# Scatter of token rows to expert slots held to two transfers under way, and one more shared block placed ahead of the expert loop

## What is computed

```python
logits = x_flat @ gate_w.T
scores = jax.nn.softmax(logits, axis=-1)
_, topk_ids = jax.lax.top_k(scores, 2)
w = scores * jax.nn.one_hot(topk_ids, E).sum(axis=1)
gu = jnp.einsum('nh,eih->nei', x_flat, experts_gate_up)
g, u = (gu[..., :I], gu[..., I:])              # I = 352, E = 8
h = jax.nn.silu(g) * u
expert_out = jnp.einsum('nei,ehi->neh', h, experts_down)
out = jnp.einsum('neh,ne->nh', expert_out, w)
shared = jax.nn.silu(x_flat @ shared_gate_w.T) * (x_flat @ shared_up_w.T) @ shared_down_w.T
shared_weight = jax.nn.sigmoid(x_flat @ shared_expert_gate_w.T)
out = out + shared_weight * shared             # width of shared: 704
# caller: x = x + tanh(g_ffn[1]) * out
```

## Time and profile before

| | us |
|---|---|
| median of three runs | 1020.92 |
| lowest and highest | 1019.35, 1020.96 |
| the profiled execution, whole | 1029.16 |
| its span, first to last instruction | 1027.0 |
| PE busy in it | 950.7 (93%) |
| DVE, ACT, POOL busy | 578.8, 482.1, 582.9 |
| mean granted TensorE clock | 0.966 |

### The profile page before, as it was taken

How to read it: one execution, slowest core, us unless ns; L and a number is a source line. 1 busy time by engine, 2 the same in 40 slices (tenths; PEclk the granted TensorE clock), 3 DMA queues, 4 the chain that set the end, 5 groups by cost and what they waited for, 6 DMA issues and landing times. The chain is left out here.

```text
span 1027.0 us, 21395 instructions
## 1 busy us (share of the span) xinstructions
PE 950.7 (93%) x7715; PEld 539.4 (53%) x7716; DVE 578.8 (56%) x1698; ACT 482.1 (47%) x661; POOL 582.9 (57%) x620
## 2 busy tenths in 40 slices
PE   6989999999996998988999999997994999999997
PEld 2644444444473554644444444464552677777754
DVE  4867888888752115776888888846331222222226
ACT  2437787887833111436877778744010122322210
POOL 3458999999834701378999999941066022222200
PEclk9978999999998998989999999998998999999999
DMA  9572838374002161464343424122722022222152
GB/s 305 183 219 44 227 64 226 65 209 82 2 22 83 43 214 37 123 138 128 64 114 64 109 54 104 27 86 110 228 78 104 17 62 62 67 62 64 44 174 82
DMA packets 87988, 107.56 MB, mean 105 GB/s; under 512 B 10528, under 2 KB 70520, under 8 KB 87896
## 3 DMA queue, kind: packets, MB, share of 16 engines
q1 hardware_dynamic: 77192, 85.08, 30.3%
q0 software_dynamic: 4848, 14.70, 4.3%
q10 hardware_dynamic: 5856, 6.56, 2.1%
HBM read 76.92 MB, written 29.38 MB: 104 GB/s over the span
## 5 line engine op out<-in xcount | busy, mean ns | idle before, releaser
L616 ACT ACTIVATE pT<-ps 128x1024 f32<-128x1024 f32 x256 | 248.4, 1022 | 98.8 <-PE ps L488 98.5
L658 POOL TENSOR_TENSOR xT<-nmax,xT 128x512 f32<-128x512 f32 x192 | 195.5, 1040 | 21.6 <-DVE nmax L556 21.3
L658 POOL TENSOR_TENSOR s<-nmax,s 128x512 f32<-128x512 f32 x192 | 196.5, 1040 | 16.8 <-DVE nmax L556 12.6
L556 DVE CUSTOM_DVE_ANT_0 s<-ps,bias 128x512 f32<-128x512 f32 x256 | 166.1, 689 | 45.2 <-PE ps L475 43.9
L556 DVE CUSTOM_DVE_ANT_0 xT<-ps,bias 128x512 f32<-128x512 f32 x256 | 166.5, 689 | 42.6 <-PE ps L475 32.3
L475 PE MATMUL ps<-ks,qs 97*128 97x512 bf16 (+1 forms) x512 | 162.5, 397 | 12.2 <-DMA ks<-qk_scratch 4.6
L503 PE MATMUL ps<-pT,vq 128*32 128x512 f32 x1024 | 135.5, 605 | 2.4
L1182 POOL DMA_INDIRECT slots_out<-y,id x39 | 38.2, 980 | 138.6 <-DVE y L1509 135.3
L475 PEld LDWEIGHTS ps<-ks,qs 97*128 97x128 bf16 (+1 forms) x512 | 30.6, 98 | 131.4 <-DVE nmax L556 65.1
L1261 PE MATMUL ps<-gu,xgT 128*128 x312 | 98.8, 460 | 0.7 <-ACT xgT L1345 0.7
L1212 PE MATMUL ps<-xT,sgu 128*128 128x512 f32 x176 | 81.2, 617 | 15.0 <-issue 10.1
(11 more groups left out here) (173 smaller groups left out, 1215.4 us busy)
## 6 DMA issues: line engine op xcount, KB each, us to landing
bias<-in_bias SPq DMA_DIRECT2D x16, 1024.0 KB, 5.9
qk_scratch<-parts SPq DMA_DIRECT2D x64, 128.0 KB
qs<-qk_scratch SPq DMA_DIRECT2D x32, 192.0 KB, 3.3
ks<-qk_scratch SPq DMA_DIRECT2D x32, 192.0 KB, 4.0
gu<-in_gate_up SPq DMA_DIRECT2D x8, 704.0 KB, 9.6
slots_in<-zeros POOLq DMA_DIRECT2D x4, 1280.0 KB, 7.1
xg<-slots_in SPq DMA_DIRECT2D x39, 130.0 KB, 2.1
qk_scratch<-parts ACTq DMA_DIRECT2D x32, 128.0 KB
```

What stands on the lines that cost most here:

```text
L556: nc.vector.tensor_tensor_reduce(at.s[m % 4][:, qt, :], sb.ps[:, ring_bank(tile_place[u - 1 + hg * 64]), :], at.bias[:, j if per_head_bias ...
L616: nc.scalar.activation(at.pT[:, slot(m // HG, m % HG), 2 * half:2 * half + 2, :], sb.ps[:, 2 + 2 * half:4 + 2 * half, :], ACT.Exp).then_in ...
L658: nc.gpsimd.tensor_tensor(s, at.nmax[:, m % 4, qt:qt + 1].to_broadcast([P, S]), s, ALU.subtract).then_inc(pool_less_max, 1)
```

## The change

`scattered` becomes two semaphores, used in turn. From the third scatter of each round on, POOL waits until the scatter before the previous one has landed, so that at most two are under way. `EARLY` becomes 2: block (1,1) moves from the late to the early ones.

```diff
-EARLY = 1
+EARLY = 2
...
-    slots_ready, scattered = sem("slots_ready"), sem("scattered")
+    slots_ready, scattered = sem("slots_ready"), [sem(f"scattered{i}") for i in range(2)]
...
-            sp.wait_ge(scattered, 16 * 2 * TT)
+            for i in range(2):
+                sp.wait_ge(scattered[i], 16 * TT)
...
             for c in range(2):
                 if c == 1:
-                    pool.wait_ge(scattered, 16 * TT)
+                    for i in range(2):
+                        pool.wait_ge(scattered[i], 16 * TT // 2)
...
                 for t in range(TT):
+                    if t >= 2:
+                        pool.wait_ge(scattered[t % 2], 16 * (c * TT // 2 + t // 2))
                     pool.indirect_dma_start(
                         out=scr.xs, out_offset=bass.IndirectOffsetOnAxis(ap=m.slot[:, c, t:t + 1], axis=0),
-                        in_=sb.tok[:, t, :], in_offset=None).then_inc(scattered, 16)
+                        in_=sb.tok[:, t, :], in_offset=None).then_inc(scattered[t % 2], 16)
```

## The result

The median of 13 runs of the changed kernel is 1013.84 us (1009.16 to 1017.91), beside 1024.1 us for 13 runs of the kernel before (1019.35 to 1027.51). The ratio is 0.9902, with a 95% interval of 0.9884 to 0.9919: 10 us faster. The forecast was 1013.5 us.

The account below looks back on a forecast made before the run. PE and its late signals during the scatters were taken to bound the stretch before the loop, PE then DVE the end. -3.0 and -8.6 gave -11.6: 1017.6 us, or 1009.4; the middle, 1013.5 us, was forecast, range 1009 to 1027.

Parts of the forecast that it names:

- The sum: Whole kernel: -3.0 us ahead of the expert loop and -8.6 us behind it, -11.6 us together.
- The end: Behind the loop: without block (1,1), DVE's last add moves from 1023.67 to 1015.10, -8.6 us.
- The front: Ahead of the loop: block (1,1) adds 13.8 us, yet without stall the first transpose starts at 807.3, not 810.3: -3.0 us.
- the holes: Idle PE time ahead of the loop that no work fills: 3.22 us at 771.17 and 10.07 us at 784.27.
- the second hole: PE's 10.07 us of idle time at 784.27, after which its granted clock was read as down to 0.50.
- The wait on POOL: Scatter stretch: two scatters take 3.2 us instead of 2.53, `xg` is there at 804.5, PE hides it: cost 0.
- The remark on an estimate of 2.3 us for one transfer: Scatter on POOL: by a fitted formula the wait would be satisfied and `xg` there 1.5 us sooner, hidden by PE.
- From the profiled execution to the median: Whole kernel: 1017.6 us like the profiled execution, or 1009.4 if its excess is spread over all work; middle 1013.5 us.
- the 8.2 us: Whole kernel: how far the earlier kernel's median lay below its profiled execution; either spread over all work or stall.
- The stall is not the scatters' number: Ahead of the loop: something else in that window causes the idle time, which stays; +5.2 us, 1026 us; chance 0.22.
- the likeliest case: Ahead of the loop: limiting scatters under way removes PE's stall; 1013.5 us, own range 1009 to 1018, chance 0.47.
- The stall belongs to the profiled execution: Ahead of the loop: timed runs lack the stall, so the change costs +3.3 us, 1024.2 us; chance 0.15.

Follow-up runs that it names:

- the block alone: Changed kernel without the wait between scatters: block (1,1) early, two semaphores in turn; 1016.03 us (1.0046 to before) on one chip, 1027.69 us (1.0066) on another.

## Why the prediction was right, point by point

**The sum.** -3.0 ahead of the loop and -8.6 behind it were forecast, -11.6; the two traces give -3.0 and -8.5, and the medians -10.3. The first transpose was forecast 57.6 us after the first scatter and came after 57.7.

**The end.** Four `expert_add` at 3.17 us in a row, then 1.7: held to a tenth. DVE now ends last, PE's last down being over at 998.5, 8 us before DVE's last adds start.

**The front.** The block costs the 13.8 us that rows of other blocks gave for it (8.58 + 5.18), and the holes with the low clock behind them gave back 16.7. One reading was loose: the earlier trace rows (792 to 794) lie in the second hole and not behind it. The clock stayed at 0.50 behind it, up to 798, and was at 0.84 from 798 to 804.

**The wait on POOL.** The term was mis-sized, without harm. I had every second scatter start 0.78 us after a landing, so that POOL would idle 0.64 us before a scatter on average. Its rows show 0.30 us, the gap without a wait, before many of them and 0.4 to 0.6 us before most others. Two scatters took 2.9 us instead of 3.2, the spacing came out at 1.45 us instead of 1.6, `xg` 52.6 us after the first scatter instead of 54.8. PE hid it either way, with 5 us to spare. The remark on an estimate of 2.3 us for one transfer gives two answers: a wait already satisfied would put `xg` at 795.2, which is 9.3 us sooner than 804.5 and not 1.5. The sum did not use it.

**From the profiled execution to the median.** This step was luck. I could not place the 8.2 us between them and took the middle, which forecast 7.4 us less than the 1020.92 then known. Measured were 10.3 us less, near the 11.6 of the sum. The two fit the same 1013.5 because the median of the kernel before rose to 1024.1 with ten more runs: the three shown are the lowest of the thirteen. The profiled 1029.16 lies above all thirteen, in part for reasons ahead of the routing (the first row of the table).

**The rivals.** "The stall is not the scatters' number" gave 1026 us with the holes staying. They went, so its forecast fell, but its name was right: it is the spacing (at 1.47 us without a limit there were none), and my reason for the likeliest case, the number under way, was wrong. My doubt stood in the prediction, that about two were under way already. Its arithmetic for holes that stay, 5.2 us slower, met 6.3 in the version with the block alone. "The stall belongs to the profiled execution" fell in the form that it had, as something that the timed runs don't share: the kernel before is 10 us slower in its median in just the comparisons whose traces show holes or lack counts. It did not fall as a cause. Every timed run here carries a span and a granted clock, so each was recorded as the profiled one was, and whether an execution that nobody records has the holes is not shown. The arithmetic of this rival describes the chips without holes. It said that without the holes the kernel before would take some 1014 us, and that the changed one would be 3.3 us slower. These chips gave 1011.4 and 1011.9, and versions with the same queue on PE 1.9 to 4.1 us more. The changed kernel itself was not run there; from the first scatter to ACT's first copy of `xg` the traces of it and of the block alone both have 58.1 us, which is why I expect the same loss of it.

**Open.** What holds up PE's signals, and why in three of the five comparisons only, no row shows. The strongest rival left is the recording itself: where signals are late, counts are missing from the record too, and a wider spacing helps both. Then the 10 us would be won in recorded executions only, and in others the change might lose its 2 to 4 us on every chip. Nothing here decides it. ACT and DVE are late for PE's semaphores and for no other, from the end of the first round of scatters on, though counts are missing from its first 4 us on. Even spacings between 1.27 and 1.47 us were not tried on a chip with holes; the changed kernel's 1.45 is a mean over starts 1.26 us to over 3 us apart.

## What to carry to other kernels

A wait for a matmul that ends long after the matmul has ended, on two engines at once, is neither PE's work nor the waiting engine's: look at what else runs from the first late release to the last, and change the rate of that. Count in the trace what must be complete, such as 16 for each transfer: where records are missing, the recording may be part of what is measured. Time such a change on more than one chip: moving a block and spacing the transfers gained 10 us in three comparisons, and versions with the same queue on PE lost 2 to 4 us in the two others. When a piece of PE's work leaves the end of a program, see which engine ends last then: here it was DVE, and filling its gaps was worth another 5.6 us in the trace.

## What the runs showed of the hardware

- Medians of the kernel before fall into two groups, with the same program: 1011.4 and 1011.9 us in two comparisons, 1021.4, 1024.1 and 1025.2 in three. Each comparison but the main one is known to be on a chip of its own, and none was repeated. In two of the slower ones the kernel before was traced: PE has 11.8 and 13.3 us of holes while POOL sends 32 indirect transfers 1.27 us apart.
- In the slower comparisons a matmul's signal came up to 12 us late (ended at 780.84, counted at 792.95), and with starts 1.45 us (by waits) or 1.47 us (by memsets) apart it came on time.
- In the same comparisons the traces hold 124 to 449 of the 512 counts of the scatters' semaphores, and all 512 in the six traces of the faster ones.
- The late signals were not slow transfers: the last scatter of the first round had landed within 2.50 us of its start in the kernel before on a chip with holes (759.10 to 761.60) and within 2.62 us in the block-only version on one without (763.44 to 766.06). Now and then one waited longer for the one before the previous one (2.30 us idle before the start at 792.27 in the changed kernel).
